# Selective scan: other step numbers for the next chunk's preparation, the z projection, the gate products, and three more u slots

## The chip, the cores and the metric

The kernel runs on one core of a Trainium2 chip. The metric is device time in microseconds (us), the median of several runs.

## The reference, cut to what matters

The reference is four layers on `x` (2 batches, 2048 rows, 512 columns): a gated selective scan ("mamba"), then one softmax attention layer and two linear attention layers. The change lies in the first layer alone. In short form it computes

```python
xn = layernorm(x) * (1 + scale) + shift
x_in, z = split(xn @ in_proj_w.T)                # 1024 channels each
u = silu(conv4(x_in) + conv_b)                    # 4 taps along the rows
dt_r, B, C = split(u @ x_proj_w.T)                # 64, 16 and 16 columns
dt = softplus(dt_r @ dt_proj_w.T + dt_proj_b)
h = h * exp(dt * A) + dt * u * B                  # row after row, 16 states a channel
y = (h * C).sum(states) + u * D_param
out = x + gate * ((y * silu(z)) @ out_proj_w.T)
```

## The kernel before, in words

`stage_mamba` cuts the 4096 rows into 8 **chunks** of 512 rows (four a batch) and the 1024 channels into 8 tiles `ct` of 128 partitions. For each chunk it walks over 64 **steps**: step i works on channel tile `ct = i // 8` and on the pair `g = i % 8` of the 16 states. Each engine has a program of its own, written out in order, that runs over the same 64 steps; semaphores keep them together, and an engine never passes an instruction that waits.

One step is this:

- VectorE (DVE): `drive` of the step ahead makes `h` = du * B for two states (L654; on the first step of a tile it makes `du` = dt * u first, L647), and then two `scan` instructions (L664) run the recurrence in place. `read_y` (L671) follows once a tile, `add_residual` (L679, L682) four times a chunk at the steps in `OUT_READ`, the row statistics of the next chunk (`norm_stats`, L611 to L622) at `STATS` and the step after.
- ScalarE (ACT): two `decay` activations make exp(dt * A) for the scans (L534) into three PSUM banks, so that ScalarE can run about one step ahead. Between them lie `softplus` of the next tile at `g == 5` (L519 to L524), `copy_z` (L539), `silu_z` (L543, with a table load before it and one after it, L546), and for the next chunk `normalise` (L462), `turn` (L469), `make_taps` (L479 to L487), `silu_u` (L499) and `split_x` (L506, L507).
- GpSimd (POOL): one product `hc` = h * C (L431, 1024 columns) and a small copy that saves the state (L433). Then what the tables put there: `gate_y`, the product y * silu(z) (L414), `add_soft` at `g == 4` (L408), `make_rstd` (L393, L395), and `add_tap`, three additions for each channel tile of the next chunk's convolution (L403): two at step `TAP[e] - 1`, one at `TAP[e]`.
- TensorE (PE): `sum_states`, which adds `hc` into y (L812), and behind it the projections that the tables put there: `project_z` (L768), `transpose_x` (L746), `project_u` (L757), `project_x` (L778), `project_dt` (L790) and `project_back` (L800).

So while a chunk is scanned, its own z, and the next chunk's rows, u and dt are made between the steps. Where each part stands is set by tables of step numbers at the head of `stage_mamba`: `STATS`, `RSTD`, `NORM`, `TR`, `IN_AT`, `TAP`, `Z_AT`, `Z_COPY`, `Z_SILU`, `GATE`, and others that the change leaves alone.

Three rings couple the engines. `h` has 3 slots: `drive(s)` waits for the product and the state copy of step s - 3. `hc` has 3 slots: the product of step s waits for `sum_states(s - 3)`. All projections share two PSUM banks (`work`) in the fixed order of the list `order`: z (8 tiles), transposes (4), u (8), x (1), out (4), then the next chunk. A use may begin when the one two places before it has been read. So the second z tile waits for `add_residual` of the last output tile of the chunk before, at step `OUT_READ[3]` = 16 of DVE, and the third z tile for `copy_z` of the first. The ring `u` is shared by the scanned chunk and the next one: `make_taps` of use n waits until `gate_y` of use n - `U_SLOTS` is done.

DMAs are issued by SP in one order: residual stores, weights, the next rows, and B and C, which are sent to DRAM and read back spread over all partitions (`spread_bc`).

Of the kernel before, what the change touches and what calls it, by code (L numbers as in the profile page):

```python
# [120 lines left out]
class Film:  # L121
# [1 line left out]

    def __init__(self, r, keep, layer, w, banks):
        self.keep, self.layer, self.w = keep, layer, w
        self.ps_row = banks[0:2]
        self.ps = banks[2][:, 0:2 * KD * NB].rearrange("p (t b) -> p t b", b=NB)
        self.row = r.sb(f"film{layer}_row", [P, 2 * D])  # L130
# [63 lines left out]
def stage_mamba(nc, a, keep, bc_dram, out):  # L194
# [4 lines left out]
    with ExitStack() as ctx:  # L199
# [2 lines left out]
        NG = N // G  # L202
        CG = CT * NG
        BC_ROWS = 2 * N
        H_SLOTS, HC_SLOTS, U_SLOTS, DA_BANKS, TAPS = 3, 3, 10, 3, CONV - 1
        TOTAL = NCH * CG

        BACK_EARLY = {58 + n: (n // 3, n % 3) for n in range(6)}
        BACK_LATE = {3: (0, 3), 4: (1, 3)} | {5 + n: (2 + n // 4, n % 4) for n in range(8)}
        Z_AT = {13 + n: divmod(n, 2) for n in range(2 * CT)}  # L210
        TR = 29
        IN_AT = {31 + n + n // 3: divmod(n, 2) for n in range(2 * CT)}
        XP_AT = {53 + n: n for n in range(4)}
        DT0, SPLIT = 58, 59
        DT_AT, READ, SOFT_AT, ADD_AT = 2, 2, 5, 4
        STATS, RSTD, NORM = 23, 24, 27
        OUT_READ = [7, 8, 12, 16]
        Z_COPY = [14 + 2 * e + 3 for e in range(CT)]
        Z_SILU = {24: (0, 1, 2), 30: (3, 4, 5), 34: (6, 7)}
        TAP = [i + 3 for i, (e, half) in IN_AT.items() if half]  # L220
        U_SILU = {TAP[3] + 1: (0, 1, 2), TAP[5] + 2: (3, 4), TAP[7] + 3: (5, 6, 7)}
        GATE = {25: 0, 27: 1, 31: 2, 35: 3, 43: 4, 51: 5, 59: 6}
        CG_AT = {3 + n: divmod(n, KC // 2) for n in range(NB * KC // 2)}
        CG_READ = 13
        GATE_LAST = 2
# [79 lines left out]
        def freed(kind, it, n):  # L305
            return work_free[seq[kind, it, n] % 2]
# [11 lines left out]
        def _(sp):  # L318
# [135 lines left out]
        def _(act):  # L454
# [272 lines left out]
        def _(pe):  # L727
# [115 lines left out]
            for it in range(NCH):  # L843
                more = it + 1 < NCH
                for i in range(CG):
# [8 lines left out]
                    if i in Z_AT:  # L854
                        project_z(it, *Z_AT[i])
# [1457 lines left out]
```

## Time and profile before

| what | value |
|---|---|
| median of 3 runs | 5495.62 us (5494.74 to 5498.09) |
| the profiled execution's own time | 5496.32 us |
| its span in the profile | 5494.5 us |
| busy: PE, DVE, ACT, POOL | 90%, 77%, 58%, 65% of the span |
| largest group of the scan stage | 512 `hc` products on POOL, 1218.1 us |
| mean granted TensorE clock | 0.972 |

The span covers all four layers. The scan stage is the first 2130 us of it. Idle time of an engine that is not the bottleneck costs nothing, so the shares by themselves say little; what matters is which wait ends last in each stretch of a chunk.

### The profile page before, as it was taken

How to read it: one execution, taken by the hardware profiler on the slowest of the kernel's cores; microseconds unless marked ns; L12 is line 12 of the kernel's file. 1: busy time of each engine (PE TensorE's matmuls, PEld its weight loads, DVE VectorE, ACT ScalarE, POOL GpSimd, SP SyncE). 2: the span in 40 equal slices, each digit the busy share in tenths (PEclk: the TensorE clock that was granted, in tenths of full speed). 3: DMA queues.
4: the chain of work that ended last, by engine and by line, in shares of the span. 5: the costliest groups of instructions: out<-in, count | busy, mean ns of one | idle time of the engine just before them, and what ended most of it. 6: DMA issues, size and time to landing. Idle time of an engine off the chain costs nothing. (4 is left out here: it accounts for less than half of the span.)

```text
span 5494.5 us, 62571 instructions
## 1 busy us (share of the span) xinstructions
PE 4941.4 (90%) x20224; PEld 2735.6 (50%) x20224; DVE 4255.5 (77%) x5657; ACT 3196.8 (58%) x5887; POOL 3594.4 (65%) x2405
## 2 busy tenths in 40 slices
PE   7888989898889877989999999999998888988998
PEld 2333333333333334864444444444443677776777
DVE  6999999999999995447777777777774565656565
ACT  3757575756666652326888888888886324232323
POOL 3879797979788874325988898888988322222222
PEclk9999999999999999997999999999998999999999
DMA  4020212212121203341111111111110412112211
GB/s 177 23 108 30 101 39 93 86 68 77 54 81 50 83 25 111 145 138 24 36 24 36 25 36 25 35 36 25 36 24 30 164 68 75 41 64 73 73 43 69
DMA packets 119638, 350.72 MB, mean 64 GB/s; under 512 B 13104, under 2 KB 14352, under 8 KB 104912
## 3 DMA queue, kind: packets, MB, share of 16 engines
q1 hardware_dynamic: 102448, 300.76, 16.4%
q0 software_dynamic: 9216, 33.56, 1.6%
q10 hardware_dynamic: 7648, 12.41, 0.7%
q8 instruction: 162, 2.65, 0.2%
q14 instruction: 164, 1.34, 0.1%
HBM read 278.49 MB, written 67.67 MB: 63 GB/s over the span
## 5 line engine op out<-in xcount | busy, mean ns | idle before, releaser
L431 POOL TENSOR_TENSOR mamba_hc<-mamba_h,mamba_bc 128x1024 f32<-128x1024 f32 x512 | 1218.1, 2379 | 360.8 <-DVE mamba_h L664 307.0
L812 PE MATMUL mamba_y<-mamba_hc,ident 128*128 128x512 f32 x2048 | 997.6, 610 | 271.9 <-POOL mamba_hc L431 269.8
L1393 POOL TENSOR_TENSOR attn_pair_sum<-attn_pair_sum,attn_prob 128x1024 f32<-128x1024 f32 x512 | 1203.9, 2385 | 56.3 <-ACT attn_prob L1508 56.3
L1552 DVE TENSOR_REDUCE attn_mx<-attn_ps_max 128x1 f32<-128x512 f32 x1536 | 967.7, 684 | 317.6 <-PE attn_ps_max L1416 313.1
L534 ACT ACTIVATE mamba_da<-mamba_dt,mamba_a_neg 128x512 f32<-128x512 f32 x1024 | 691.1, 689 | 722.2 <-DVE mamba_h L664 718.6
L1508 ACT ACTIVATE attn_prob<-attn_ps_s 128x512 f32<-128x512 f32 x2048 | 1051.3, 602 | 78.5 <-PE attn_ps_s L1443 78.4
L664 DVE TENSOR_TENSOR_SCAN mamba_h<-mamba_da,mamba_state,mamba_h 128x512 f32<-128x512 f32 x768 | 940.3, 1266 | 1.9 <-ACT mamba_da L534 1.9
L1443 PE MATMUL attn_ps_s<-attn_q_stack,attn_k_stack 100*128 100x512 f32 x2048 | 885.3, 436 | 5.2 <-ACT attn_prob L1508 5.2
L1416 PE MATMUL attn_ps_max<-attn_k_stack,attn_q_stack 98*128 98x512 f32 x2048 | 833.3, 412 | 37.5 <-DMA attn_q_stack<-qk_parts 19.7
L812 PEld LDWEIGHTS mamba_y<-mamba_hc,ident 128*128 128x128 f32 x2048 | 366.1, 191 | 856.1 <-POOL mamba_hc L431 459.2
L654 DVE TENSOR_TENSOR mamba_h<-mamba_du,mamba_bc 128x1024 f32<-128x1024 f32 x512 | 619.9, 1211 | 64.6 <-POOL mamba_state L433 56.8
L1443 PEld LDWEIGHTS attn_ps_s<-attn_q_stack,attn_k_stack 100*128 100x128 f32 x2048 | 386.2, 189 | 516.4 <-ACT attn_prob L1508 381.9
L1454 PE MATMUL attn_ps_o<-attn_prob,attn_v_h 128*32 128x512 f32 x4096 | 547.4, 607 | 1.1 <-POOL attn_v_h L1366 1.1
L1517 ACT ACTIVATE attn_own_exp<-attn_ps_max,attn_own_neg 128x512 f32<-128x512 f32 x512 | 352.3, 688 | 283.7 <-DVE attn_own_neg L1552 280.2
L1416 PEld LDWEIGHTS attn_ps_max<-attn_k_stack,attn_q_stack 98*128 98x128 f32 x2048 | 396.1, 195 | 147.4 <-DVE attn_mx L1552 41.6
L1393 POOL TENSOR_TENSOR attn_pair_sum<-attn_prob 128x1024 f32<-128x1024 f32 x128 | 302.1, 2383 | 139.8 <-ACT attn_prob L1508 139.8
L1552 DVE TENSOR_REDUCE attn_own_neg<-attn_ps_max 128x1 f32<-128x512 f32 x512 | 348.7, 681 | 0.2 <-PE attn_ps_max L1416 0.2
L664 DVE TENSOR_TENSOR_SCAN mamba_h<-mamba_da,mamba_zeros,mamba_h 128x512 f32<-128x512 f32 x256 | 313.5, 1266 | 0.8 <-ACT mamba_da L534 0.8
L800 PE MATMUL mamba_work<-mamba_w,mamba_zy 128*128 128x512 f32 x512 | 251.3, 617 | 31.6 <-DVE mamba_x_in L682 31.1
L957 POOL TENSOR_TENSOR lin_xn_second<-lin_norm_x,lin_xn_first 128x512 fp32r<-128x512 f32 x64 | 83.7, 1339 | 293.2 <-DVE lin_norm_x L2123 275.6
L757 PE MATMUL mamba_work<-mamba_xn_t,mamba_w 128*128 128x512 f32 x512 | 241.9, 599 | 1.0 <-ACT mamba_xn_t L469 0.9
L768 PE MATMUL mamba_work<-mamba_xn_t,mamba_w 128*128 128x512 f32 x512 | 242.3, 595 | 0.0
(336 smaller groups left out, 7447.1 us busy)
## 6 DMA issues: line engine op xcount, KB each, us to landing
mamba_bc<-bc_dram SPq DMA_DIRECT2D x64, 1024.0 KB, 7.2
mamba_w<-in_in_proj_w_T SPq DMA_DIRECT2D x16, 2048.0 KB, 7.6
qk_parts<-qkv_pair POOLq DMA_DIRECT2D x64, 512.0 KB, 3.2
attn_k_stack<-qk_parts SPq DMA_DIRECT2D x96, 256.0 KB
attn_q_stack<-qk_parts SPq DMA_DIRECT2D x96, 256.0 KB
mamba_x_in<-in_x SPq DMA_DIRECT2D x16, 1024.0 KB, 5.7
mamba_w<-in_out_proj_w_T SPq DMA_DIRECT2D x8, 2048.0 KB, 8.3
lin_norm_x<-x_after_L SPq DMA_DIRECT2D x16, 1024.0 KB, 5.7
```

The source lines that it names most:

```text
L431: nc.gpsimd.tensor_tensor(hc[:, gs % HC_SLOTS, :, :], h[:, gs % H_SLOTS, :, :], bc[:, g, G:2 * G, :], ALU.mult).then_inc(s["hc_done"], 1)
L534: nc.scalar.activation(da[n % DA_BANKS][:, :], dt[:, ct % 2, :], ACT.Exp, scale=a_neg[:, ct, g * G + j:g * G + j + 1]).then_inc(s["exp_don ...
L654: nc.vector.tensor_tensor(h[:, gs % H_SLOTS, :, :], du[:, :].unsqueeze(1).to_broadcast([P, G, CH]), bc[:, g, 0:G, :], ALU.mult).then_inc(s ...
L664: nc.vector.tensor_tensor_scan(h[:, gs % H_SLOTS, j, :], da[(gs * G + j) % DA_BANKS][:, :], h[:, gs % H_SLOTS, j, :], first, ALU.mult, ALU ...
L812: mm = nc.tensor.matmul(y[ct % 2][:, :], ident[:, :], hc[:, gs % HC_SLOTS, j, :], start=(g == 0 and j == 0), stop=(g == NG - 1 and j == G ...
L1393: nc.gpsimd.tensor_tensor(pair_sum[(hd * NGRP + g) % 2][:, at], first[:, at], prob[unit % SLOTS][:, at], ALU.add).then_inc(s["sum_done"], 1)
L1416: nc.tensor.matmul(free_bank(seq)[:, :].rearrange("p (a j) -> p a j", j=P), q_st[slot][0:ROWS_MAX, qt * P:(qt + 1) * P], k_st[slot][0:ROWS ...
L1443: nc.tensor.matmul(ps_s[n % BANKS][:, :], k_st[slot][0:ROWS, kt * P:(kt + 1) * P], q_st[slot][0:ROWS, c * CH:(c + 1) * CH], start=True, st ...
L1454: mm = nc.tensor.matmul(ps_o[c * DH1:(c + 1) * DH1, :], v_h[hd % 3][:, kt, :], prob[kt % SLOTS][:, c * CH:(c + 1) * CH], start=(kt == 0), ...
L1508: nc.scalar.activation(prob[kt % SLOTS][:, c * CH:(c + 1) * CH], ps_s[n % BANKS][:, :], ACT.Exp).then_inc(s["exp_done"], 1)
L1517: nc.scalar.activation(own_exp[:, :], ps_max[seq % BANKS][:, :], ACT.Exp, bias=own_neg[hd % 3][:, i // QB, :], accum_out=own_sum[hd % 3][: ...
L1552: nc.vector.tensor_reduce(to, ps_max[seq % BANKS][:, :], AX.X, ALU.max, negate=own_block(i)).then_inc(s["bank_read"], 1)
```

## The change

It renumbers steps. For the next chunk the statistics begin at step 19 in place of 23 (`RSTD` 20 for 24, `NORM` 22 for 27), the transposes at 24 in place of 29, and the sixteen halves of `project_u` stand at steps 26 to 51 in place of 31 to 51, so that `TAP` becomes 30, 34, 37, 40, 44, 47, 50, 54 in place of 35, 38, 40, 43, 46, 48, 51, 54. The sixteen halves of `project_z` stand in the eleven steps 13 to 23 (two in every other step or so) in place of one in each of 13 to 28; the silus of z move to 20, 25 and 31 from 24, 30 and 34. Of the gate products, tiles 0 to 2 move to 22, 23, 27 and tiles 3 to 6 from 35, 43, 51, 59 to 57, 58, 59, 61. The u ring gets 13 slots for 10, for which room is made by laying two tiles of the set-up (`film` row and wide) into `hc`. `split_x` becomes one activation on 96 partitions into one tile `xp_rows` in place of two.

```diff
-        H_SLOTS, HC_SLOTS, U_SLOTS, DA_BANKS, TAPS = 3, 3, 10, 3, CONV - 1
+        H_SLOTS, HC_SLOTS, U_SLOTS, DA_BANKS, TAPS = 3, 3, 13, 3, CONV - 1
...
-        Z_AT = {13 + n: divmod(n, 2) for n in range(2 * CT)}
-        TR = 29
-        IN_AT = {31 + n + n // 3: divmod(n, 2) for n in range(2 * CT)}
+        Z_AT = [(13 + 2 * n // 3, *divmod(n, 2)) for n in range(2 * CT)]
+        TR = 24
+        IN_AT = {26 + 5 * n // 3: divmod(n, 2) for n in range(2 * CT)}
...
-        STATS, RSTD, NORM = 23, 24, 27
+        STATS, RSTD, NORM = 19, 20, 22
...
-        Z_COPY = [14 + 2 * e + 3 for e in range(CT)]
-        Z_SILU = {24: (0, 1, 2), 30: (3, 4, 5), 34: (6, 7)}
+        Z_COPY = [step + 3 for step, e, half in Z_AT if half]
+        Z_SILU = {20: (0, 1, 2), 25: (3, 4, 5), 31: (6, 7)}
...
-        GATE = {25: 0, 27: 1, 31: 2, 35: 3, 43: 4, 51: 5, 59: 6}
+        GATE = {22: 0, 23: 1, 27: 2, 57: 3, 58: 4, 59: 5, 61: 6}
...
-                nc.scalar.activation(dt_r[:, :], bank[0:RANK, :], ACT.Copy).then_inc(s["xp_read"], 1)
-                nc.scalar.activation(bc_rows[:, :], bank[RANK:RANK + BC_ROWS, :], ACT.Copy).then_inc(freed("xp", it, 0), 1)
+                nc.scalar.activation(xp_rows[:, :], bank[0:RANK + BC_ROWS, :], ACT.Copy).then_inc(freed("xp", it, 0), 1)
```

On PE, at steps 12 to 17 of the first chunk, L812 is `sum_states` (a row with x2 is one step) and L768 is `project_z` (x2 is one half). Before:

```order
L812 MATMUL mamba_y<-mamba_hc,ident 128x512 x6
L768 MATMUL mamba_work<-mamba_xn_t,mamba_w 128x512 x2
L812 MATMUL mamba_y<-mamba_hc,ident 128x512 x2
L768 MATMUL mamba_work<-mamba_xn_t,mamba_w 128x512 x2
L812 MATMUL mamba_y<-mamba_hc,ident 128x512 x2
```

and now:

```order
L812 MATMUL mamba_y<-mamba_hc,ident 128x512 x6
L768 MATMUL mamba_work<-mamba_xn_t,mamba_w 128x512 x4
L812 MATMUL mamba_y<-mamba_hc,ident 128x512 x2
L768 MATMUL mamba_work<-mamba_xn_t,mamba_w 128x512 x2
L812 MATMUL mamba_y<-mamba_hc,ident 128x512 x2
L768 MATMUL mamba_work<-mamba_xn_t,mamba_w 128x512 x4
```

Two halves now stand between two sums in five of the eleven steps, so the sum of the step behind them comes later in the queue.

On ACT, around the first group of z silus of the first chunk (L539 `copy_z`, L534 `decay`, L543 the silus, L519 to L524 `softplus`). Before, the silus stand at step 24, and no softplus follows before step 29:

```order
L539 ACTIVATE mamba_zy<-mamba_work 128x512
L534 ACTIVATE mamba_da<-mamba_dt,mamba_a_neg 128x512 x2
L543 ACT_TABLE_LOAD
L543 ACTIVATE mamba_zy<-mamba_zy 128x512 x3
L546 ACT_TABLE_LOAD
L534 ACTIVATE mamba_da<-mamba_dt,mamba_a_neg 128x512 x2
L539 ACTIVATE mamba_zy<-mamba_work 128x512
```

and now, at step 20, right behind the copy of the fourth z tile and ahead of the softplus of step 21:

```order
L539 ACTIVATE mamba_zy<-mamba_work 128x512
L543 ACT_TABLE_LOAD
L543 ACTIVATE mamba_zy<-mamba_zy 128x512 x3
L546 ACT_TABLE_LOAD
L534 ACTIVATE mamba_da<-mamba_dt,mamba_a_neg 128x512 x2
L519 ACTIVATE mamba_dt<-mamba_y,cols 128x512
L520 ACTIVATE mamba_soft<-mamba_y,cols 128x512
L522 ACTIVATE mamba_soft<-mamba_soft 128x512
L524 ACTIVATE mamba_soft<-mamba_soft 128x512
```

The decays of step 21 and that softplus now queue behind the silus.

On POOL, from the first tap pair on (L403 is L404 in the changed file, a tap addition; L414 a gate product; L408/L409 `add_soft`). Before, steps 34 to 37:

```order
L403 TENSOR_TENSOR mamba_u<-mamba_u,mamba_tap 128x512 x2
L431 TENSOR_TENSOR mamba_hc<-mamba_h,mamba_bc 128x1024
L433 COPY mamba_state<-mamba_h 128x2
L414 TENSOR_TENSOR mamba_zy<-mamba_u,mamba_zy 128x512
L403 TENSOR_TENSOR mamba_u<-mamba_u,mamba_tap 128x512
L431 TENSOR_TENSOR mamba_hc<-mamba_h,mamba_bc 128x1024
L433 COPY mamba_state<-mamba_h 128x2
L408 TENSOR_TENSOR mamba_dt<-mamba_dt,mamba_soft 128x512
```

and now, steps 33 to 36:

```order
L404 TENSOR_TENSOR mamba_u<-mamba_u,mamba_tap 128x512 x2
L432 TENSOR_TENSOR mamba_hc<-mamba_h,mamba_bc 128x1024
L434 COPY mamba_state<-mamba_h 128x2
L404 TENSOR_TENSOR mamba_u<-mamba_u,mamba_tap 128x512
L432 TENSOR_TENSOR mamba_hc<-mamba_h,mamba_bc 128x1024
L434 COPY mamba_state<-mamba_h 128x2
L432 TENSOR_TENSOR mamba_hc<-mamba_h,mamba_bc 128x1024
L434 COPY mamba_state<-mamba_h 128x2
L409 TENSOR_TENSOR mamba_dt<-mamba_dt,mamba_soft 128x512
```

The gate product is gone from between the taps, and a free step lies between one tile's taps and the next.

## Rows read from the trace of the kernel before

**Rows 1.** Busy time by stretch (start:end, length, PE, PEld, DVE, ACT, POOL, clock, DMA): quiet, then taps.
```profile
620.00:640.00 20.00, 20.00 (x47) 8.47 (x46) 19.93 (x20) 8.77 (x14) 13.26 (x11) 1.00 0.08 27
978.00:1052.00 74.00, 58.60 (x128) 22.71 (x127) 66.43 (x58) 57.66 (x110) 72.67 (x59) 1.00 0.00 0
```
**Rows 2.** Waits in the chunk from 841 to 1097 us: total us, times, longest.
```profile
DVE mamba_h L654 <- POOL mamba_state L433: 8.1, 7, 1.5
```
**Rows 3.** Line L393 (once a chunk), 100 to 2100 us: duration min/median/max, first and last start.
```profile
L393 POOL TENSOR_TENSOR mamba_rstd<-mamba_var_eps,neg_half x7: 1017/1017/1022, 173.7 to 1709.8; 128x4 f32<-128x4 f32 x7
```
**Rows 4.** Timeline of DVE, 898 to 948 us: start, length, engine, line, operation, tiles, count.
```profile
903.83 1.20 DVE L654 TENSOR_TENSOR mamba_h<-mamba_du,mamba_bc 128x1024 f32<-128x1024 f32 x1
904.94 2.45 DVE L664 TENSOR_TENSOR_SCAN mamba_h<-mamba_da,mamba_state,mamba_h 128x512 f32<-128x512 f32 x2
907.31 0.67 DVE L679 TENSOR_TENSOR mamba_work<-mamba_work,gate 128x512 f32<-128x512 f32 x1
...
908.62 1.21 DVE L654 TENSOR_TENSOR mamba_h<-mamba_du,mamba_bc 128x1024 f32<-128x1024 f32 x1
...
915.60 0.72 DVE L671 SCALAR_TENSOR_TENSOR mamba_u<-mamba_u,cols,mamba_y 128x512 f32<-128x512 f32 x1
...
930.18 0.68 DVE L647 TENSOR_TENSOR mamba_du<-mamba_dt,mamba_u 128x512 f32<-128x512 f32 x1
...
934.40 1.26 DVE L611 BATCH_NORM_STATS2 mamba_stats<-mamba_x_in 128x6 f32<-128x512 f32 x2
935.58 1.21 DVE L654 TENSOR_TENSOR mamba_h<-mamba_du,mamba_bc 128x1024 f32<-128x1024 f32 x1
...
939.07 1.26 DVE L611 BATCH_NORM_STATS2 mamba_stats<-mamba_x_in 128x6 f32<-128x512 f32 x2
...
940.78 0.82 DVE L621 TENSOR_SCALAR mamba_neg_mean<-mamba_mv 128x4 f32<-128x4 f32 x1
```
**Rows 5.** Timeline of POOL, in the taps.
```profile
980.61 2.69 POOL L403 TENSOR_TENSOR mamba_u<-mamba_u,mamba_tap 128x512 f32<-128x512 f32 x2
983.25 2.34 POOL L431 TENSOR_TENSOR mamba_hc<-mamba_h,mamba_bc 128x1024 f32<-128x1024 f32 x1
...
985.68 1.27 POOL L414 TENSOR_TENSOR mamba_zy<-mamba_u,mamba_zy 128x512 f32<-128x512 f32 x1
```
**Rows 6.** Timeline of DVE, in the taps.
```profile
994.22 1.84 DVE L647 TENSOR_TENSOR mamba_du<-mamba_dt,mamba_u 128x512 f32<-128x512 f32 x1
```
**Rows 7.** Timeline of PE, first half of the second z tile and the sum behind it.
```profile
909.22 1.88 PE L768 MATMUL mamba_work<-mamba_xn_t,mamba_w 128*128 128x512 f32 x4
910.93 1.88 PE L812 MATMUL mamba_y<-mamba_hc,ident 128*128 128x512 f32 x4
```
**Rows 8.** Timeline of ACT, softplus and the first silus of z.
```profile
922.79 0.67 ACT L519 ACTIVATE mamba_dt<-mamba_y,cols 128x512 f32<-128x512 f32 x1
...
925.27 0.58 ACT L539 ACTIVATE mamba_zy<-mamba_work 128x512 f32<-128x512 f32 x1
...
934.05 1.28 ACT L543 ACT_TABLE_LOAD   x1
...
938.33 1.30 ACT L534 ACTIVATE mamba_da<-mamba_dt,mamba_a_neg 128x512 f32<-128x512 f32 x2
```
**Rows 9.** Timeline of POOL at step 24 of that chunk.
```profile
939.23 2.35 POOL L431 TENSOR_TENSOR mamba_hc<-mamba_h,mamba_bc 128x1024 f32<-128x1024 f32 x1 [2.18 <-DVE mamba_h L664]
...
941.75 1.02 POOL L393 TENSOR_TENSOR mamba_rstd<-mamba_var_eps,neg_half 128x4 f32<-128x4 f32 x1
942.85 0.20 POOL L395 TENSOR_TENSOR mamba_shift<-mamba_neg_mean,mamba_rstd 128x4 f32<-128x4 f32 x1
```
**Rows 10.** The page's DMA issues: tiles, queue, operation, count, KB, median us to landing.
```profile
mamba_x_in<-in_x SPq DMA_DIRECT2D x16, 1024.0 KB, 5.7
```
**Rows 11.** Timeline of PE: the longest wait of the same chunk, and what follows it.
```profile
872.13 3.38 PE L800 MATMUL mamba_work<-mamba_w,mamba_zy 128*128 128x512 f32 x4 [4.45 <-DVE mamba_x_in L682]
...
947.64 1.98 PE L812 MATMUL mamba_y<-mamba_hc,ident 128*128 128x512 f32 x4 [2.25 <-POOL mamba_hc L431]
```

More of the change, by code:

```diff
@@ L121, with __init__ @@
 class Film:
-    def __init__(self, r, keep, layer, w, banks):
+    def __init__(self, r, keep, layer, w, banks, row=None, wide=None):
         self.keep, self.layer, self.w = keep, layer, w
@@ L129, in __init__ @@
         self.ps = banks[2][:, 0:2 * KD * NB].rearrange("p (t b) -> p t b", b=NB)
-        self.row = r.sb(f"film{layer}_row", [P, 2 * D])
-        self.wide = r.sb(f"film{layer}_wide", [P, KC, PT])
+        self.row = r.sb(f"film{layer}_row", [P, 2 * D]) if row is None else row
+        self.wide = r.sb(f"film{layer}_wide", [P, KC, PT]) if wide is None else wide
         self.widened = r.sem(f"film{layer}_widened")
@@ L241, in stage_mamba @@
         zy = r.sb("zy", [P, CT, CH])
-        dt_r = r.sb("dt_r", [RANK, CH])
-        bc_rows = r.sb("bc_rows", [BC_ROWS, CH])
+        xp_rows = r.sb("xp_rows", [RANK + BC_ROWS, CH])
+        dt_r, bc_rows = xp_rows[0:RANK, :], xp_rows[RANK:RANK + BC_ROWS, :]
         bc = r.sb("bc", [P, NG, 2 * G, CH])
@@ L267, in stage_mamba @@
         silu = keep["silu"]
-        film = Film(r, keep, 0, film_w, da)
+        film = Film(r, keep, 0, film_w, da, hc[:, 0, :, :].rearrange("p g t -> p (g t)"),
+                    hc[:, 1, 0, 0:KC * PT].rearrange("p (k n) -> p k n", k=KC))
         fa, fb = keep["film"][:, 0, 0], keep["film"][:, 0, 1]
@@ L271, in stage_mamba @@
                  "drive_done exp_done scan_done state_saved hc_done sum_done y_read gated z_done tap_done tap_added u_done "
-                 "xp_read bc_written out_gated residual_in stored own_act own_norm setup_done zero_done "
+                 "bc_written out_gated residual_in stored own_act own_norm setup_done zero_done "
                  "u_begun gate_b_in cond_in small_in gate_w_in silu_done ident_done neg_done sum_set")
@@ L348, in spread_bc @@
                         sp.wait_ge(bc_in[g], it * 16)
-                sp.dma_start(bc_dram.rearrange("(r t) -> r t", t=CH), bc_rows[:, :]).then_inc(s["bc_written"], 16)
+                sp.dma_start(bc_dram.rearrange("(r t) -> r t", t=CH), bc_rows).then_inc(s["bc_written"], 16)
                 sp.wait_ge(s["bc_written"], (it + 1) * 16)
@@ L786, in project_dt @@
                 if ct == 0:
-                    pe.wait_ge(s["xp_read"], it + 1)
+                    wait_freed(pe, "xp", it, 0)
                 if n >= 2:
                     pe.wait_ge(s["y_read"], n - 1)
-                nc.tensor.matmul(y[ct % 2][:, :], w_dt[:, ct * P:(ct + 1) * P], dt_r[:, :], start=True, stop=True
+                nc.tensor.matmul(y[ct % 2][:, :], w_dt[:, ct * P:(ct + 1) * P], dt_r, start=True, stop=True
                                  ).then_inc(s["dt_full"], 1)
@@ L853, in _ @@
                         project_back(it - 1, *BACK_LATE[i])
-                    if i in Z_AT:
-                        project_z(it, *Z_AT[i])
+                    for step, e, half in Z_AT:
+                        if i == step:
+                            project_z(it, e, half)
                     if more:
```

## The prediction

> **What bounds the kernel now.** I read first the busy time by stretch, then the waits of one chunk, then the timelines engine by engine. E(s) below is the moment at which DVE has ended the two scans of step s.
>
> In a quiet stretch of the scan stage DVE is busy 19.93 of 20 us and POOL 13.26: DVE is the bound. In the stretch of the taps it turns: POOL 72.67 of 74 us, DVE 66.43 [rows 1]. In one chunk `drive` waits 8.1 us for POOL's state copy, nearly the whole idle time of DVE there [rows 2]. A chunk lasts (1709.8 - 173.7) / 6 = 256.0 us [rows 3].
>
> What DVE would need alone follows from [rows 4]: a step is 907.31 - 903.83 = 3.48 us (drive 1.11, two scans 2.37), one residual 1.31, `du` 0.68, the statistics 1.18 and 940.78 + 0.82 - 939.07 = 2.53. With 0.64 for each `read_y` (0.72 less the 0.08 by which one row's end overlaps the next start), a chunk has 64 x 3.48 + 8 x 0.68 + 8 x 0.64 + 4 x 1.31 + 3.71 = 242.2 us; with the few hundredths between instructions I take 242.7. So a middle chunk loses 13.3 us, more than the idle time shows: in the taps `du` takes 1.84 [rows 6] in place of 0.68, because it starts while POOL works and gets its second SBUF operand only when POOL's operation has ended. The same is seen against a product: `neg_mean` takes 0.82 for four columns and ends with the product that began at 939.23 [rows 4, 9].
>
> **The change, part by part.** POOL's operations follow one another at 2.30 (product) and 0.14 (copy), 1.23 for a gate or soft addition and 2.64 for a tap pair [rows 5]. A step costs POOL 2.44, DVE 3.48. `drive` of step s + 3 needs the copy of step s, so POOL may be about 0.9 late before DVE waits.
>
> *Taps and gates, by sum.* Before, steps 34 to 54: POOL 21 x 2.44 + 8 x (2.64 + 1.23) + three soft additions and three gates at 1.23 = 89.6; DVE 21 x 3.48 + 3 x 0.68 + 3 x 0.64 = 77.0. The excess, 12.6, is near the 13.3 lost. Now, steps 29 to 54: POOL 26 x 2.44 + 31.0 + 3.7 = 98.1, DVE 94.4: excess 3.7. This is the lower bound of the loss. The upper one is what leaving out three gates alone gives: 13.3 - 3.7 = 9.6.
>
> *By walk.* The sum misses bunching: a pair makes POOL 2.64 - 1.04 = 1.6 late at once. So I carried both queues forward step by step with these durations, a release taken as 0.06, and `du` held while a POOL operation is in flight. Over the old table this gives a chunk of 256.1 and a loss of 13.5. Over the new one, losses behind the taps of the eight tiles: 1.22 (`du` of step 32 held 0.72, two drives 0.50); 0.19; 1.96 (softplus and taps stand in the same ACT step 37, scan 38 waits 0.87; `du` 0.70; drives 0.39); 0.54; 0.66; 1.42; 0.73; 0.94. Behind the taps four gates stand at 57, 58, 59, 61, each 1.23 against a spare of 1.04; the last is in flight when the next chunk's first `du` comes: 0.62. Sum 8.3, nearer to the upper bound since the bunching is there in the old rows too. **Gain 13.5 - 8.3 = 5.2 in each of the seven chunks with taps: 36.4 us.**
>
> *z in eleven steps.* PE needs 1.72 for a half and as much for a sum (910.93 - 909.22) [rows 7], so a step with two halves takes it 5.2 against DVE's 3.48. Worse, the second z tile may not begin before the residual at step 16 has freed its bank, 1.31 after E(16), that is 908.62. In the old order that tile begins at 909.22, behind the sum of step 15: just in time. In the new order it stands behind the sum of step 14, one sum less, so PE gets there at 907.5 and waits 1.2. From 908.7 on nine operations lie up to the end of the fourth tile (six halves, sums 15 to 17): 908.7 + 9 x 1.72 = 924.2. The first silu group now stands behind that tile's copy at ACT step 20: copy 0.5, load to next decay 938.33 - 934.05 = 4.28, decay 0.65 [rows 8], so scan 21 finds its decay at 929.7. DVE is at E(20) = 907.31 + 17.1 = 924.4 (four steps, the residual, one `read_y`, the first statistics), then 2.53 and 1.11: ready at 928.0. **It waits 1.65.** Next softplus, 925.27 - 922.79 = 2.48 [rows 8], delays decay 22: 0.26. POOL's soft addition of step 20 waits for that softplus, to 932.8; behind it queue `make_rstd`, 1.3 (942.85 + 0.20 - 941.75) [rows 9], and product 21, which starts at 935.4 while `du` of step 24 is due at 935.8: `du` is held for the rest of that product, 1.84, and drive 24 0.20. Sum 3.95 in a middle chunk. For `du` the bounds are 0 (it comes first) and 2.30 (a whole product); the timing puts it near the upper.
>
> The last chunk has no statistics to cover: E(20) is 1.17 earlier and no 2.53 follows, so scan 21 waits 5.35; with the later waits (0.26, 0.54, 0.20, 0.50) 6.85. The first chunk has no residuals and PE is early: `du` 0.89 and drive 0.20 only. **Cost 6 x 3.95 + 6.85 + 1.1 = 31.7 us.**
>
> *The rest.* The earlier statistics must find their rows loaded. That load starts when the last residual, 908.62, is stored, and lands 5.7 us after its issue [rows 10]; E(19) is 3 x 3.48 + 0.64 = 11.1 after 908.62, which leaves 5.4 for the store. I cost it at nothing; if that cover is gone, the statistics (L611) wait. The merged `split_x` saves one ACT operation of about 0.58 a chunk, the length of the copy in [rows 8], behind the last silus of u: at most 4 us in all, taken as nothing. The tiles laid into `hc` touch the set-up alone.
>
> **Sum.** -36.4 + 31.7 = -4.7 on the profiled execution's 5496.3: 5491.6. The median of the runs is 0.7 lower, so I predict **5491 us**. From no change a measurement of this kernel tells about 0.2%, 11 us.
>
> **The new wait on PE.** It is 1.2 us long and may have a price of its own. After an idle 4.45 us four matmuls took 3.38 in place of 1.88; after 2.25 us the four took 1.98 [rows 11]. The wait is shorter than the second row's, so I add nothing. The Trainium skill, page "TensorE: Matmul & The Clock Gate", section "What's actually happening", says that the array's clock is gated by how busy the engine has lately been, and an idle stretch drops it from 2.4 to 1.2 GHz. By that rule the new wait could bring the slow clock, and the sum would be the second rival's 5501 in place of 5491; the row after 2.25 us speaks against it.
>
> **The rivals.**
> - *z is hidden after all (faster).* If `du` of step 24 comes before product 21 (0.4 us decide), the middle chunk's cost falls by 1.84 + 0.20 to 1.9, the total to 19.4, and the time is 5479. If the silus fit as well, only the 36.4 remain: 5459. For it: the margins are tenths of a us. Against: in the walk POOL waits 5.9 us for the softplus, far more than tenths. Chance 0.30 for a gain over 11 us.
> - *The clock falls at the new wait.* Then z tile four is 1.5 later (3.38 - 1.88) in seven chunks: +10.5, 5501. Against: the second of [rows 11]. Chance 0.08, still within 0.2%.
> - *`du` waits for a train (slower).* POOL now works back to back around six `du` of a chunk. If `du` does not get in after one operation but has to let the next go too, that is four taps at 1.3, one product of 2.4 and one of 2.3, 9.9, less 1.2 of drives that it would cover: 8.7 x 7 = 61, time 5552. It decides where two POOL operations are ready without a gap. Against: in [rows 6] 1.84 - 0.68 = 1.16 is one operation, though a tap pair stood ready. The Trainium skill, page "SBUF — State Buffer", section "SBUF: two separate sides", has the shared port locked by one instruction as a whole and the loser blocked until then; it says nothing of trains, and by it this rival falls. Chance 0.04.
> - *The taps gain only the three gates,* 3.7 x 7 = 26, and the clock falls too: -26 + 42 = +16, 5511. Chance 0.05.
> - *The change does not do what it says:* were the ring still short, taps would wait for gates. With 13 slots the last tile needs gate 2, at step 27; none waits. No chance of its own.
>
> **How the numbers follow.** Forecast with the second rival 0.60 (within 0.2%), faster 0.30, slower 0.10 (train, gates alone, and mishaps of that size). The range of the forecast alone is 5480 to 5502. To hold 8 in 10 it goes down into the first rival, past 5479, to 5471, and up to 5503.
>
> **What would show it.** Right: `drive`'s wait for the state copy falls from 8.1 to some 3 in a chunk; scans wait for decay at step 21, 1.65 in middle chunks and over 5 in the last; POOL waits about 6 us for softplus at step 20; `du` of step 24 lasts over 2 us; a chunk lasts 254.5 to 255. Wrong: no scan waits at step 21, or a chunk under 253 (z hidden) or over 257 (a train), or PE with slow matmuls behind the wait for L682 at step 14.

## The result, and the profile after

The changed kernel takes **5507.92 us** (median of 15 runs, 5492.49 to 5512.04) against 5495.65 us for the kernel before (15 runs, 5486.07 to 5501.63): ratio 1.0019, 95% interval 1.0012 to 1.0026. It is 12 us slower where 5491 was forecast, and the time lies 5 us above the range, which ended at 5503. The profiled execution has a span of 5507.7 us (before 5494.5), mean granted TensorE clock 0.969 (before 0.972).

Where the 13.2 us of the two spans lie follows from the ends of the scans (L664): a chunk is counted from the end of its predecessor's last scan to the end of its own.

| us | before | after | difference | forecast |
|---|---|---|---|---|
| start, to the first step's end | 81.7 | 83.8 | +2.1 | 0 |
| first chunk, steps 1 to 63 | 247.7 | 247.4 | -0.4 | -4.1 |
| six middle chunks | 1536.1 | 1539.8 | +3.7 | -7.5 |
| last chunk | 237.5 | 244.6 | +7.1 | +6.9 |
| behind the scans | 3391.6 | 3392.1 | +0.5 | 0 |

The forecasts are the prediction's own terms: 1.1 - 5.2 for the first chunk, 3.95 - 5.2 for a middle one, 6.85 for the last. The last chunk came out as worked out. The miss lies in the others, and there not in all alike: the six middle chunks took 255.5, 256.9, 257.8, 257.1, 255.4 and 257.0 us, while before all six took 256.0. (Over the profiles of this study the start varies by up to 4 us and the rest by up to 7, also between kernels with the same code there.)

**The waits of DVE.** Views of the changed kernel: DVE's waits in the chunk from 1358.5 us, a good one (first two lines), then the decay waits of a bad one, from 843.5, and of the last chunk. They answer to [rows 2]: total, times, longest.

```profile
DVE mamba_h L664 <- ACT mamba_da L534: 2.9, 2, 2.0
DVE mamba_h L654 <- POOL mamba_state L434: 2.3, 6, 0.8
...
DVE mamba_h L664 <- ACT mamba_da L534: 5.5, 2, 3.5
...
DVE mamba_h L664 <- ACT mamba_da L534: 6.2, 2, 5.7
```

`drive`'s wait for the state copy fell from 8.1 to 2.3 or 2.4 in every middle chunk (some 3 was forecast). So the taps did gain. What came instead are waits for decay, and they differ between chunks.

**z, step 21, in the good chunk.** Timelines of the changed kernel, by engine: PE at the second z tile, ACT at the first silus, then DVE and POOL.

```profile
1425.81 1.98 PE L768 MATMUL mamba_work<-mamba_xn_t,mamba_w 128*128 128x512 f32 x4 [0.82 <-DVE mamba_x_in L682]
...
1441.56 0.60 ACT L539 ACTIVATE mamba_zy<-mamba_work 128x512 f32<-128x512 f32 x1 [3.36 <-PE mamba_work L768]
1442.17 1.28 ACT L543 ACT_TABLE_LOAD   x1
...
1446.45 1.30 ACT L534 ACTIVATE mamba_da<-mamba_dt,mamba_a_neg 128x512 f32<-128x512 f32 x2
...
1447.17 2.46 DVE L664 TENSOR_TENSOR_SCAN mamba_h<-mamba_da,mamba_state,mamba_h 128x512 f32<-128x512 f32 x2 [2.00 <-ACT mamba_da L534]
...
1450.33 1.27 POOL L409 TENSOR_TENSOR mamba_dt<-mamba_dt,mamba_soft 128x512 f32<-128x512 f32 x1 [6.23 <-ACT mamba_soft L524]
...
1453.24 2.47 DVE L647 TENSOR_TENSOR mamba_du<-mamba_dt,mamba_u 128x512 f32<-128x512 f32 x1
```

Link by link this is the chain of the prediction: PE waits for the residual (0.82 shown, 1.2 forecast), the fourth z tile is copied at 1441.56, the silus follow, scan 21 waits 2.00 (1.65 forecast), POOL waits 6.23 for softplus (5.9), and `du` of step 24 takes 2.47 (0.68 + 1.84 = 2.52). In the last chunk scan 21 waits 5.7 (5.35).

**The clock in the taps.** What the prediction did not have is in the busy time by stretch, steps 35 to 41 of the seven chunks with taps (start:end, length, PE, PEld, DVE, ACT, POOL, PEclk, DMA share, GB/s). The kernel before, first and last chunk:

```profile
209.90:239.00 29.10, 22.44 (x49) 8.43 (x47) 27.34 (x24) 21.71 (x45) 28.47 (x23) 1.00 0.00 0
...
1745.90:1775.00 29.10, 22.47 (x49) 8.43 (x47) 27.37 (x24) 21.73 (x44) 28.43 (x23) 1.00 0.00 0
```

and the changed kernel:

```profile
214.50:244.00 29.50, 23.87 (x46) 9.09 (x44) 26.54 (x23) 18.98 (x36) 27.38 (x22) 0.88 0.00 0
472.80:500.90 28.10, 21.13 (x46) 7.86 (x44) 26.75 (x24) 20.40 (x39) 27.42 (x22) 1.00 0.00 0
728.30:756.50 28.20, 22.16 (x46) 8.58 (x44) 26.83 (x24) 19.01 (x37) 27.42 (x22) 0.94 0.00 1
985.30:1015.70 30.40, 24.34 (x46) 8.71 (x44) 26.47 (x23) 20.53 (x39) 27.41 (x22) 0.89 0.00 0
1243.10:1271.40 28.30, 22.24 (x46) 8.61 (x44) 26.80 (x23) 19.00 (x37) 27.39 (x22) 0.94 0.00 0
1500.20:1528.20 28.00, 21.07 (x46) 7.86 (x44) 26.69 (x23) 20.32 (x39) 27.32 (x22) 1.00 0.00 0
1755.60:1783.80 28.20, 22.22 (x46) 8.62 (x44) 26.80 (x24) 18.98 (x37) 27.35 (x22) 0.94 0.00 0
```

The instructions are the same in each (the counts differ only by what the edges of a stretch cut off). Where the clock is 1.00, the chunk is one of the two quick ones (255.4, 255.5); where it is below, TensorE ran a stretch at the lower of its two levels, 1.2 GHz, and the chunk is one of the slow ones. The longer the stretch (0.89), the slower the chunk (257.8).

The single runs point the same way, with the same instructions in each: of the changed kernel's 15, the twelve with a mean granted clock of 0.968 to 0.970 took 5505.2 to 5512.0 us, the three with 0.971 or 0.972 took 5492.5 to 5502.4, while the 29 runs of the kernel before beside e1 to e4 show no such order (5487.7 us at 0.967, 5501.5 at 0.966). A mean over all four layers does not by itself place the difference in the taps.

**How the slow clock reaches the scans.** Timeline of PE in the changed kernel: the sum of step 37 and the second half of u tile 3 behind it, first in the bad chunk at 745, then in the good one at 1517.

```profile
744.97 3.56 PE L812 MATMUL mamba_y<-mamba_hc,ident 128*128 128x512 f32 x4 [2.48 <-POOL mamba_hc L432]
748.36 1.88 PE L757 MATMUL mamba_work<-mamba_xn_t,mamba_w 128*128 128x512 f32 x4
...
1516.82 1.98 PE L812 MATMUL mamba_y<-mamba_hc,ident 128*128 128x512 f32 x4 [2.45 <-POOL mamba_hc L432]
1518.64 1.88 PE L757 MATMUL mamba_work<-mamba_xn_t,mamba_w 128*128 128x512 f32 x4
```

Timeline of ACT, the same two places (L480 begins `make_taps` of tile 3, L534 is decay, L500 the first three silus of u), and DVE's scan 42 in the bad chunk:

```profile
750.28 0.78 ACT L480 ACTIVATE mamba_u<-mamba_work,cols 128x512 f32<-128x512 f32 x1 [1.50 <-PE mamba_work L757]
...
753.27 1.32 ACT L534 ACTIVATE mamba_da<-mamba_dt,mamba_a_neg 128x512 f32<-128x512 f32 x2
754.61 1.28 ACT L500 ACT_TABLE_LOAD   x1
...
758.88 2.73 ACT L534 ACTIVATE mamba_da<-mamba_dt,mamba_a_neg 128x512 f32<-128x512 f32 x4
...
759.61 2.46 DVE L664 TENSOR_TENSOR_SCAN mamba_h<-mamba_da,mamba_state,mamba_h 128x512 f32<-128x512 f32 x2 [1.26 <-ACT mamba_da L534]
...
1520.57 0.76 ACT L480 ACTIVATE mamba_u<-mamba_work,cols 128x512 f32<-128x512 f32 x1
```

The sum takes 3.56 in place of 1.98 us. The half behind it ends 1.5 late, ACT waits those 1.50 us with `make_taps`, and the decay of step 42 stands behind two table loads and three silus, 758.88 - 754.61 = 4.27 us in which ACT can make up nothing. Scan 42 waits. Laid beside the good chunk step by step, the three bad chunks at 0.94 differ by over 0.15 us in nothing but steps 41 and 42 (up to 0.26, and 1.37), the one at 0.89 in nothing but steps 38 (2.58 longer) and 39 (0.20 shorter). There the slow stretch met `project_dt` (L790), which took 2.07 in place of 1.12 (the second row, from a stretch at full clock), and softplus, which shares its ACT step with taps, waited for it:

```profile
991.91 2.07 PE L790 MATMUL mamba_y<-mamba_xp_rows,mamba_w_dt 64*128 64x512 f32 x2
...
1443.17 1.12 PE L790 MATMUL mamba_y<-mamba_xp_rows,mamba_w_dt 64*128 64x512 f32 x2
...
994.02 0.69 ACT L519 ACTIVATE mamba_dt<-mamba_y,cols 128x512 f32<-128x512 f32 x1 [1.37 <-PE mamba_y L790]
```

So there are two statements to test: that the clock causes these waits and follows from how PE's work is spread (theory **clock**), against the rival that softplus, taps and silus in one place of ACT cause them and the clock only accompanies them (**order**); and beside it the size of the two terms that the prediction did have.

### The profile page after: what moved, and what is told of

Read it like the earlier page. It is cut to its first block and busy times, and to the rows that moved or that the text cites. A ratio compares the mean times of both kernels' runs of the same rounds, so it can differ in the third digit from the quotient of the medians.

```text
span 5507.7 us, 62560 instructions
## 1 busy us (share of the span) xinstructions
PE 4953.8 (90%) x20224; PEld 2744.9 (50%) x20224; DVE 4274.4 (78%) x5657; ACT 3189.7 (58%) x5879; POOL 3596.2 (65%) x2405
## 5 line engine op out<-in xcount | busy, mean ns | idle before, releaser
L812 PE MATMUL mamba_y<-mamba_hc,ident 128*128 128x512 f32 x2048 | 1001.9, 613 | 275.7 <-POOL mamba_hc L432 274.0
L534 ACT ACTIVATE mamba_da<-mamba_dt,mamba_a_neg 128x512 f32<-128x512 f32 x1024 | 686.1, 688 | 630.3 <-DVE mamba_h L664 626.3
L664 DVE TENSOR_TENSOR_SCAN mamba_h<-mamba_da,mamba_state,mamba_h 128x512 f32<-128x512 f32 x768 | 939.8, 1265 | 26.6 <-ACT mamba_da L534 25.8
L812 PEld LDWEIGHTS mamba_y<-mamba_hc,ident 128*128 128x128 f32 x2048 | 372.7, 192 | 856.2 <-POOL mamba_hc L432 447.1
L664 DVE TENSOR_TENSOR_SCAN mamba_h<-mamba_da,mamba_zeros,mamba_h 128x512 f32<-128x512 f32 x256 | 313.3, 1265 | 7.9 <-ACT mamba_da L534 7.8
L768 PE MATMUL mamba_work<-mamba_xn_t,mamba_w 128*128 128x512 f32 x512 | 235.6, 595 | 3.7 <-DVE mamba_x_in L682 3.7
## 6 DMA issues: line engine op xcount, KB each, us to landing
attn_k_stack<-qk_parts SPq DMA_DIRECT2D x96, 256.0 KB
attn_q_stack<-qk_parts SPq DMA_DIRECT2D x96, 256.0 KB
```

What stands on the lines that cost most here:

```text
L534: nc.scalar.activation(da[n % DA_BANKS][:, :], dt[:, ct % 2, :], ACT.Exp, scale=a_neg[:, ct, g * G + j:g * G + j + 1]).then_inc(s["exp_don ...
L664: nc.vector.tensor_tensor_scan(h[:, gs % H_SLOTS, j, :], da[(gs * G + j) % DA_BANKS][:, :], h[:, gs % H_SLOTS, j, :], first, ALU.mult, ALU ...
L812: mm = nc.tensor.matmul(y[ct % 2][:, :], ident[:, :], hc[:, gs % HC_SLOTS, j, :], start=(g == 0 and j == 0), stop=(g == NG - 1 and j == G ...
```

## The experiments

Seven kernels, each timed beside the kernel before on the same chip: e1 to e4 on one (kernel before: 5496.77 us), e5 to e7 on another (5494.49).

**e1 and e2: the same halves, with and without ten more matmuls.** Both move five first halves of u a step later. e1 also issues, at the steps in `BUSY` and behind `project_u`, a matmul whose result is overwritten, so PE has more to do and nothing else changes; e2 has `IN_AT` alone.

```diff
-        IN_AT = {26 + 5 * n // 3: divmod(n, 2) for n in range(2 * CT)}
+        IN_AT = {step: divmod(n, 2) for n, step in enumerate(
+            [26, 27, 30, 31, 33, 34, 36, 37, 40, 41, 43, 44, 46, 47, 50, 51])}
+        BUSY = {28: 1, 29: 1, 32: 2, 35: 3, 38: 4, 39: 4, 42: 5, 45: 6, 48: 7, 49: 7}
...
+            def keep_busy(it, e):
+                begin("in", it, e)
+                nc.tensor.matmul(at("in", it, e)[:, :], w_view("in", it)[:, 0, e * P:(e + 1) * P], xn_t[:, 0, :],
+                                 start=True, stop=True)
```

> The changed kernel with ten more matmuls of the u projection in steps 28 to 49 of each of seven chunks (each repeats a first matmul whose result is overwritten; PE computes nothing new), placed in steps that had a sum alone; five first halves move one step later, every second half and so every tap stays in its step. Theory 'clock': the changed kernel lost because TensorE, with its sixteen halves spread over 26 steps, stands idle more between them, its clock fell to half at step 36 or 39 in five of seven chunks, and the taps and decays behind came late (scan waits of 1.4 us at step 42 in three chunks, 2.4 at step 38 in one, 3.3 in all in the first chunk). Then no stretch at half clock lies in steps 26 to 52, those waits are gone, each middle chunk lasts 255.4 us and the time falls by about 10 us, 5507.9 to 5497 (5494 to 5500). Theory 'order': the waits at 38 and 42 come from softplus and taps standing in the same ScalarE step, the clock only accompanies them; then they stay, and the time stays within 5505 to 5511.

> The control of the first run: the same five first halves moved one step later, without the ten matmuls. No work is added or left out. Theory 'clock': the idle share of TensorE is that of the changed kernel, so its clock still falls in the taps of most chunks, and the time is within 5 us of the changed kernel's, 5503 to 5513. If the moved halves and not the ten matmuls were what helps, this kernel would be as fast as the first run, about 5497. Theory 'order': no difference, 5505 to 5511.

Measured: **e1 5498.51 us** (11 runs; ratio to before 1.0005, interval 0.9996 to 1.0013), **e2 5509.39** (7 runs; 1.0027, 1.0016 to 1.0038). With more work on PE the kernel is 10.9 us quicker than without it; by the lengths of the chunks in the two profiles it is 10.7. Busy time of steps 35 to 41 in e1, the second and the fourth chunk:

```profile
468.60:497.00 28.40, 23.89 (x53) 9.19 (x51) 26.71 (x24) 21.63 (x43) 27.72 (x22) 1.00 0.00 1
...
980.80:1008.80 28.00, 22.82 (x51) 8.77 (x49) 26.70 (x23) 20.29 (x39) 27.31 (x22) 1.00 0.00 1
```

and in e2:

```profile
469.50:499.40 29.90, 23.12 (x48) 8.99 (x46) 26.82 (x23) 21.54 (x44) 28.29 (x22) 0.94 0.00 0
...
984.50:1014.60 30.10, 23.34 (x49) 9.14 (x47) 26.83 (x23) 21.75 (x45) 28.27 (x22) 0.93 0.00 0
```

The sum of step 37, which took 3.56 us in the chunk shown above, in the same chunk of e1 (L819 there), and the busy time of e1 at steps 41 to 43 of that chunk:

```profile
741.53 1.98 PE L819 MATMUL mamba_y<-mamba_hc,ident 128*128 128x512 f32 x4 [1.61 <-POOL mamba_hc L434]
...
750.00:762.00 12.00, 9.68 (x19) 3.93 (x18) 11.37 (x11) 7.81 (x11) 10.22 (x9) 0.86 0.00 0
```

In e1 the clock is 1.00 in steps 35 to 41 in all seven chunks, no middle chunk has the waits at 38 and 42, and all six take 255.9 to 256.3 us. In e2 three of them take 258.9 to 259.1. Theory "clock" holds and "order" falls: the order on ACT is the same in both. One part of what was expected is wrong: the clock is not at 1.00 everywhere in e1's steps 26 to 52. It falls at step 42 of the six middle chunks and at step 31 of two of them, but there it costs only 0.33 (steps 45 to 47) and 0.35 us (step 36). In the first chunk it falls at steps 32 and 51 and costs 2.0 (steps 36, 55 and 56). The Trainium skill, page "TensorE: Matmul & The Clock Gate", section "What's actually happening", has the clock set by how busy the array has recently been; e1 against e2 agrees, with 10.9 us between them. Where in a chunk the clock falls is not told by the wait ahead of it: the two sums of the changed kernel shown above waited 2.48 and 2.45 us, and only the first was slow.

**e3: the gates alone.** All tables as before, but 13 slots and gates 3 to 6 behind the taps.

```diff
-        GATE = {25: 0, 27: 1, 31: 2, 35: 3, 43: 4, 51: 5, 59: 6}
+        GATE = {25: 0, 27: 1, 31: 2, 57: 3, 58: 4, 59: 5, 61: 6}
```

> One part of the change alone: 13 slots of u and gates 3 to 6 at steps 57, 58, 59, 61; statistics, z, transposes, u halves and the silus stand as in the kernel before, gates 0 to 2 too. By the same walk as in the prediction a chunk with taps lasts 253.95 in place of 256.1 us, so the time falls by 7 x 2.2 = 15 us, to 5480 (5476 to 5486); TensorE's halves stand as before, so theory 'clock' expects no stretch at half clock in the taps. If the gates were no cost where they stood (POOL late for another reason), the time is that of the kernel before, 5495; if gates behind the taps hold up the output projection or the next chunk's first du, over 5500.

Measured: **5481.34 us** (11 runs; 0.9973, 0.9964 to 0.9982). Waits of DVE in the chunk from 1091.6 us:

```profile
DVE mamba_h L654 <- POOL mamba_state L434: 4.9, 5, 1.5
DVE mamba_h L664 <- ACT mamba_da L534: 0.4, 1, 0.4
```

and the busy time of e3 at steps 37 and 38 of another chunk:

```profile
981.00:990.00 9.00, 8.41 (x16) 3.72 (x17) 8.64 (x8) 6.73 (x15) 9.00 (x9) 0.81 0.00 0
```

`drive` waits 4.9 in place of the 8.1 of [rows 2], and a middle chunk takes 254.2 to 254.6 (253.95 by the walk). One part of the change alone is 15 us faster than the kernel before, and 27 us faster than the whole change. By the chunks of the two profiles it is 11.8 faster than the kernel before; another 4.9 lies behind the scans, where the code is the same, so it is in part luck that the forecast time was met so closely. The expectation on the clock was wrong here too: it falls at steps 26 or 27 and at 37 in every second middle chunk, though the halves of u stand as before, and costs at most 0.4 us.

**e7: the rest alone.** The change with those gates back at 35, 43, 51 and 59.

```diff
-        GATE = {22: 0, 23: 1, 27: 2, 57: 3, 58: 4, 59: 5, 61: 6}
+        GATE = {22: 0, 23: 1, 27: 2, 35: 3, 43: 4, 51: 5, 59: 6}
```

> The change without the moved gates of tiles 3 to 6, which stand at 35, 43, 51 and 59 again (13 slots, early rows and z in eleven steps stay). By the walk a chunk with taps is 3.0 us longer than in the change: 7 x 3.0 = 21, 5529 (5522 to 5536); the z waits at step 21 as in the change. It is the complement of the third run: if parts add, the moved gates are worth 15 us in the old surroundings and 21 in the new, and the rest of the change costs 27 to 33. If the gates' place does not matter once the rows begin early, 5508.

Measured: **5521.69 us** (5 runs; 1.0050, 1.0037 to 1.0062). A chunk with taps is some 2.5 us longer than in the change (first chunk 249.0 for 247.4, middle 258.6 to 260.3 for 255.4 to 257.8), less than the walk's 3.0. The clock falls at step 35 or 36 in all seven of these chunks, so the difference is not the gates' price alone. Together with e3 this makes a square: by the times the moved gates are worth 15 us in the old surroundings (5496.8 to 5481.3) and 14 in the new (5521.7 to 5507.9), and the rest of the change (early rows, z in eleven steps) costs 26 to 27. By the chunks of the four profiles the gates are worth 12 and 18, and the rest costs 22 and 28. So the parts add to within some us; how well is not settled, because each of these kernels meets the slow clock at other steps.

**e4: the bank of the second z tile.** The fourth residual one step earlier.

```diff
-        OUT_READ = [7, 8, 12, 16]
+        OUT_READ = [7, 8, 12, 15]
```

> The changed kernel with the fourth residual of a chunk at step 15 in place of 16; nothing else moves. The z price of the prediction: the second z tile waits for the bank that this residual frees. Then TensorE's wait at step 14 falls from 1.2 to about 0, z tile four is ready 1 us sooner, scan 21's wait falls from 2.0 to below 1 in middle chunks and from 5.7 to 4.4 in the last, du of step 24 is still held about 1.4; by the walk a chunk with residuals is 1.3 us shorter, 7 x 1.3 = 9 us: 5499 (5496 to 5503), the clock in the taps unchanged. Rival: the z chain is set by something else (the silus' length alone), then scan 21 waits as before and the time stays at 5508.

Measured: **5501.67 us** (11 runs; 1.0010, 1.0001 to 1.0019), 6.3 less than the change (4.4 by the chunks of the two profiles). The first half of the second z tile and scan 21 of the chunk that was shown above, timelines of PE and DVE:

```profile
1419.66 1.88 PE L768 MATMUL mamba_work<-mamba_xn_t,mamba_w 128*128 128x512 f32 x4
...
1440.93 2.46 DVE L664 TENSOR_TENSOR_SCAN mamba_h<-mamba_da,mamba_state,mamba_h 128x512 f32<-128x512 f32 x2 [0.90 <-ACT mamba_da L534]
```

The wait fell from 2.00 to 0.90, and PE no longer waits for the residual. Step 21 is 1.1 shorter (1.3 was expected), and the last chunk 1.05. The time fell less than 9, because now the clock falls at step 39 in all six middle chunks, at 1.63 us each (steps 41 and 42), where the change had it in three.

**e5: the silus of u one step later.** e4 with one number more.

```diff
-        U_SILU = {TAP[3] + 1: (0, 1, 2), TAP[5] + 2: (3, 4), TAP[7] + 3: (5, 6, 7)}
+        U_SILU = {TAP[3] + 2: (0, 1, 2), TAP[5] + 2: (3, 4), TAP[7] + 3: (5, 6, 7)}
```

> The fourth run (fourth residual at step 15) with one table number more: the first three silus of u stand at ScalarE step 42 in place of 41. In the fourth run the clock fell at step 39 of every middle chunk and cost 0.26 + 1.37 us at steps 41 and 42. Theory: a slow sum of step 37 makes project_u's second half of tile 3 end 1.5 us late, ScalarE waits for it with make_taps, and since the silus (two table loads and three silus, 4.3 us) stand directly behind, decay 42 comes late; with the silus one step later the decays of step 42 pass ahead of them and the same slow clock costs nothing. Then the waits at 41 and 42 go, a middle chunk lasts 254.4 in place of 256.06 us, and the time falls by about 7 x 1.6 = 11 us from 5501.7 to 5490 (5487 to 5496), although the half-clock stretches in the taps stay (they may move, since the chunk is shorter: one at step 36 would cost up to 2.6 a chunk and take the time to 5503). Rival: TensorE's slow clock costs the time through the sums (hc slots, read_y), not through ScalarE's order; then the time stays at 5499 to 5503 with the waits at 41 and 42 or beside them.

Measured: **5501.05 us** (11 runs; 1.0014, 1.0005 to 1.0023): no gain over e4 (6.6 us over the kernel before on its chip, e4 4.9 on its own), so the expected time is missed by 11 us. The mechanism is seen all the same. Timelines of e5 in the third chunk: the slow sum on PE, ACT's `make_taps`, decays and silus, then scan 42.

```profile
739.98 3.39 PE L812 MATMUL mamba_y<-mamba_hc,ident 128*128 128x512 f32 x4 [2.47 <-POOL mamba_hc L432]
...
745.41 0.78 ACT L480 ACTIVATE mamba_u<-mamba_work,cols 128x512 f32<-128x512 f32 x1 [1.62 <-PE mamba_work L757]
...
748.41 2.75 ACT L534 ACTIVATE mamba_da<-mamba_dt,mamba_a_neg 128x512 f32<-128x512 f32 x4
751.18 1.28 ACT L500 ACT_TABLE_LOAD   x1
...
753.39 2.45 DVE L664 TENSOR_TENSOR_SCAN mamba_h<-mamba_da,mamba_state,mamba_h 128x512 f32<-128x512 f32 x2
```

The sum is slow, ACT waits 1.62, four decays pass ahead of the silus, and scan 42 waits for nothing. Step 42 is 1.36 us shorter than in e4 in all middle chunks; the 0.26 at step 41 stays wherever the sum of step 37 is slow, against what was expected. But the chunks now meet the clock elsewhere: in three of them it falls at step 35 and costs 1.3 at step 38; and step 21 is 0.7 to 1.1 longer in all six. Beside that stands a longer slow stretch at steps 7 and 8, ahead of z. Busy time there in e4:

```profile
612.00:626.00 14.00, 10.20 (x20) 4.50 (x21) 13.93 (x14) 4.15 (x6) 7.97 (x7) 0.88 0.10 37
```

and in e5:

```profile
608.50:622.50 14.00, 9.83 (x18) 4.32 (x19) 13.93 (x15) 4.15 (x6) 7.96 (x7) 0.76 0.10 37
```

The one leads to the other by way of z. Counted from the end of step 12, the first half of z begins 0.7 to 1.0 us later in e5's middle chunks than in e4's (11.94 for 11.23 in the third), and the copy of the fourth tile and step 21 come later by as much. In three chunks of the change the slow stretch is as long and z begins 0.6 to 0.9 later too, but there the tile has to wait for the residual anyway. What lengthened the stretch is not shown. By chunks e5 is still 2.3 us shorter than e4; start and rest, which no table touches, took it back.

**e6: z, rows, gates and silus placed anew.** Gates behind the taps, z in thirteen steps with its silus behind a softplus, one tile's taps every three steps.

```diff
-        Z_AT = [(13 + 2 * n // 3, *divmod(n, 2)) for n in range(2 * CT)]
-        TR = 24
-        IN_AT = {26 + 5 * n // 3: divmod(n, 2) for n in range(2 * CT)}
+        Z_AT = [(13 + 4 * n // 5, *divmod(n, 2)) for n in range(2 * CT)]
+        TR = 26
+        IN_AT = {28 + 3 * n // 2: divmod(n, 2) for n in range(2 * CT)}
...
-        STATS, RSTD, NORM = 19, 20, 22
-        OUT_READ = [7, 8, 12, 16]
+        STATS, RSTD, NORM = 20, 21, 23
+        OUT_READ = [7, 8, 12, 15]
...
-        Z_SILU = {20: (0, 1, 2), 25: (3, 4, 5), 31: (6, 7)}
+        Z_SILU = {22: (0, 1, 2), 27: (3, 4, 5), 34: (6, 7)}
...
-        U_SILU = {TAP[3] + 1: (0, 1, 2), TAP[5] + 2: (3, 4), TAP[7] + 3: (5, 6, 7)}
-        GATE = {22: 0, 23: 1, 27: 2, 57: 3, 58: 4, 59: 5, 61: 6}
+        U_SILU = {TAP[3] + 2: (0, 1, 2), TAP[5] + 2: (3, 4), TAP[7] + 3: (5, 6, 7)}
+        GATE = {24: 0, 25: 1, 27: 2, 56: 3, 57: 4, 58: 5, 59: 6}
```

> A version put together from what the runs showed: gates behind the taps (56 to 59) and 13 slots as in the change; z in thirteen steps (13 to 25) in place of eleven, with the silus of z behind a softplus and not ahead of it (22, 27, 34), the fourth residual at 15, statistics at 20, transposes at 26, u halves at 28 to 50, one tile's taps every three steps, the first silus of u one step later. By the walk of the prediction a middle chunk lasts 250.6 us (against 256.1 before and 255.0 for the change), the last 1.4 more than before, and the scan stage 37.6 us less than before: 5459. With the clock falling in the taps of every chunk for 0.6 to 2 us more each: up to 5473. Expected 5463 (5456 to 5476). If the z price (a scan waiting for its decay at step 21) stays although its order is mended, 5485 or more.

Measured: **5466.31 us** (5 runs; 0.9950, 0.9937 to 0.9962), 28 us under the kernel before; each taken against the kernel before on its own chip, that is some 40 under the change and 13 under e3. Waits of DVE in its third chunk:

```profile
DVE mamba_h L654 <- POOL mamba_state L434: 2.3, 6, 0.8
DVE mamba_h L664 <- ACT mamba_da L534: 0.9, 1, 0.9
```

The drives wait as little as in the change, the decay wait is 0.9 in place of 2.9 to 5.5. A middle chunk takes 251.2 to 252.5 (250.6 by the walk). That it is the early rows which gain against e3, now that z does not pay for them, is likely and not shown: e6 differs from e3 in the rows, z, the residual and the silus at once.

## Why the prediction was wrong

- **What failed: the full clock in every chunk's taps.** Each PE operation of the sums and the walk stood at its time at full clock, and the one place where a fall was looked for was the new wait for the residual ("I add nothing"). [rows 1] show 1.00 in the taps before, and that was carried over to a table in which PE has sixteen halves in 26 steps instead of 21. Measured: the four chunks with a clock below 1.00 are 1.5, 2.4, 1.7 and 1.6 us longer than the good one, and the first is 2.6 longer than in e5 (247.4 against 244.8), where one fall is left that costs 0.3. That is **10.0 us** that no term held, and e1 against e2 (10.9 us) shows the clock as the cause of such waits. That the spread of the halves alone brought the falls is not shown: e3 has falls with the halves as before, though cheap ones. A bound was at hand: the first of [rows 11] prices four matmuls at half clock at 1.5 us more, seven chunks make 10.5, and the range should have reached to 5491 + 10.5 and more, not have this as a rival with 0.08 at one place.
- **The criterion was wrong as well.** The forecast took it from [rows 11] that a wait shorter than 2.25 us leaves the clock up, so that only the new wait needed looking at. The same sum of step 37 waits 2.48 and 2.45 in two chunks, and falls in one. At the new wait of z, to which the criterion was applied, the clock did not fall: the second tile's first half took 1.98 in all six chunks in which PE waits there.
- **Rival two and the fourth rival.** The time that rival two gave, +10.5, has the right size and the wrong place. The fourth, which ended at 5511, is the nearest to the time, but not by its ways: the taps gained more than the gates alone (e3: 15 us, 11.8 by its chunks; the taps of the change, without the clock, some 4.8 us in each of seven chunks, 34 us).
- **Taps and gates: right, a little high.** Steps 26 to 63 of a good middle chunk are 4.8 us shorter than before (255.43 - 256.00, less the 4.22 of z), 5.2 were forecast. The gate left in flight at the chunk's end costs 0.65 at step 63 (0.62 forecast). For the gates alone the same walk gave 5480 and e3 measured 5481.34, but a chunk gained 1.4 to 1.8 and not 2.15: the walk is some 0.4 high here as well.
- **z in eleven steps: right.** Steps 20 to 25 are 4.22 us longer (3.95 forecast), in the first chunk 1.5 (1.1), the last chunk 7.1 (6.85). e4 shows the first link, the bank. In e6, with thirteen steps, silus behind the softplus and the residual at 15 together, 0.1 to 1.4 us of the 4.22 are left in middle chunks and 3.1 of the 7.1 in the last.
- **`du` and a train of POOL operations.** `du` of step 24 at 2.47 is one product's hold. In all eight chunks no `du` takes more than 2.48, so no train was seen. Three chunks did last over 257 us, which the prediction gave as a train's sign; there it was the clock.
- **The sum.** The chunks came out at +10.5 against -4.7. Of these 15.2, the clock is 10.0; z 0.27 in each of six chunks and 0.3 in the last, 1.9; the taps 0.4 in each of six, 2.4; the first chunk's remainder 0.9 (244.5, e5's without the 0.3 of its fall, against 247.7 - 4.1). The 2.6 of start and rest beside it are of the size by which profiles of one code differ.

## What to carry to other kernels

Leaving an engine less busy is not free when its clock depends on how busy it is (10.9 us between e1 and e2): price it with rows at either clock level, in every stretch where its share of work falls, and look who waits for it there. The same slow sum cost 1.6 us where ACT had two table loads and silus right behind, and 0.3 where four decays stood ahead of them; so leave room behind each wait that may come late. And split a change before judging it: here, by the times, one part was worth 15 us and the other cost 27, and the whole showed only their difference.

## What was not expected of the hardware

Chunks with the same instructions do not repeat alike: with the changed table the clock fell in the taps in five of seven chunks, at steps 36 or 39 or both, in the kernel before in none, in e4 at step 39 of each middle chunk. Shortening a chunk by a us or two moved the falls (e4 to e5), so one edit changed costs at places that it did not touch; what decides the place was not settled here.

Two engines also hold each other both ways: while `du` took 2.47 us next to POOL's product, POOL's state copy behind that product took 0.65 in place of 0.18. Timeline of POOL in the changed kernel:

```profile
1455.10 0.65 POOL L434 COPY mamba_state<-mamba_h 128x2 f32<-128x2 f32 x1
...
1458.01 0.18 POOL L434 COPY mamba_state<-mamba_h 128x2 f32<-128x2 f32 x1
```
